# Self-attention over image pixels on one core: shift rows sent from other queues

## The reference

```python
xf = x.reshape(B, Cc, N)                      # x: (4, 256, 32, 32), so N = 1024
q = jnp.einsum('oc,bcn->bon', Wq, xf) + bq[None, :, None]     # 32 x 1024
k = jnp.einsum('oc,bcn->bon', Wk, xf) + bk[None, :, None]     # 32 x 1024
v = jnp.einsum('oc,bcn->bon', Wv, xf) + bv[None, :, None]     # 256 x 1024
scores = jnp.einsum('bqi,bqj->bij', q, k)
attn = jax.nn.softmax(scores, axis=-1)
out = jnp.einsum('bcj,bij->bci', v, attn)
return out.reshape(B, Cc, W, H) + x
```

## Time and profile before

| | us |
|---|---|
| median of 3 runs (lowest, highest) | 170.4 (170.19, 170.5) |
| the profiled execution | 170.36 |
| its span, first to last instruction | 168.5 |
| TensorE matmul busy | 160.3 (95%) |
| VectorE busy | 138.5 (82%) |
| ScalarE busy | 107.2 (64%) |
| GpSimd busy | 49.7 (29%) |

### The profile page before, as it was taken

The page is one execution under the profiler, slowest core; times in us unless marked ns, Lnnn a source line. Parts: engine busy times, 40 slices in busy tenths (PEclk is TensorE's granted clock), DMA queues, the critical chain, the costliest instruction groups (busy, mean ns, idle before and its releaser), DMA issues. The chain is left out here.

```text
span 168.5 us, 2430 instructions
## 1 busy us (share of the span) xinstructions
PE 160.3 (95%) x786; PEld 131.1 (78%) x786; DVE 138.5 (82%) x220; ACT 107.2 (64%) x196; POOL 49.7 (29%) x65
## 2 busy tenths in 40 slices
PE   7978999999999999999999999999999999999990
PEld 5567978797887898798787898798787898767870
DVE  1879899898979999899979999897979879854552
ACT  3658896836997646757896646736895636755210
POOL 6399630170235300420235300420235300214300
PEclk9999999999999999999999999999999999999999
DMA  5932465063312030251311130251311130003003
GB/s 182 352 120 78 128 196 224 0 156 83 131 44 66 28 124 0 51 138 52 124 47 57 41 126 0 55 134 47 127 48 55 42 124 0 5 0 124 0 0 126
DMA packets 7949, 14.48 MB, mean 86 GB/s; under 512 B 1672, under 2 KB 2240, under 8 KB 7936
## 3 DMA queue, kind: packets, MB, share of 16 engines
q1 hardware_dynamic: 6656, 13.37, 24.4%
q0 software_dynamic: 864, 0.82, 2.3%
q10 hardware_dynamic: 416, 0.13, 0.3%
HBM read 4.59 MB, written 4.19 MB: 52 GB/s over the span
## 5 line engine op out<-in xcount | busy, mean ns | idle before, releaser
L818 PE MATMUL acc<-w_hi,v_hi 128*128 128x512 f32 x128 | 51.2, 400 | 0.0
L818 PE MATMUL acc<-w_hi,v_lo 128*128 128x512 f32 x128 | 50.4, 393 | 0.0
L439 ACT ACTIVATE w_full<-st 128x512 f32<-128x512 f32 x64 | 37.8, 592 | 10.5 <-PE st L804 10.5
L406 ACT ACTIVATE dump<-slot,negmax 128x1024 f32<-128x1024 f32 x29 | 32.4, 1118 | 12.8 <-DVE negmax L548 12.4
L826 PE MATMUL acc<-w_lo,v_hi 128*128 128x512 f32 x120 | 38.7, 398 | 0.4 <-POOL w_lo L326 0.2
L603 DVE TENSOR_TENSOR w_lo<-w_full,w_hi 128x512 fp32r<-128x512 f32 x48 | 33.2, 693 | 5.7 <-ACT w_full L439 1.9
L548 DVE TENSOR_REDUCE negmax<-slot 128x1 f32<-128x1024 f32 x29 | 35.3, 1217 | 1.8 <-PE slot L739 1.8
L326 POOL TENSOR_TENSOR w_lo<-w_full,w_hi 128x512 fp32r<-128x512 f32 x16 | 20.7, 1291 | 47.5 <-ACT w_full L439 47.4
L818 PEld LDWEIGHTS acc<-w_hi,v_hi 128*128 128x128 f32 x128 | 24.2, 189 | 7.1 <-DVE x_sb L612 1.2
L818 PEld LDWEIGHTS acc<-w_hi,v_lo 128*128 128x128 f32 x128 | 24.2, 189 | 5.3
L826 PEld LDWEIGHTS acc<-w_lo,v_hi 128*128 128x128 f32 x120 | 22.3, 188 | 7.0 <-POOL w_lo L326 2.1
(11 more groups left out here) (84 smaller groups left out, 187.9 us busy)
## 6 DMA issues: line engine op xcount, KB each, us to landing
out<-x_sb SPq DMA_DIRECT2D x7, 512.0 KB, 2.8
x_sb<-x SPq DMA_DIRECT2D x3, 1024.0 KB, 5.5
k_b<-k_a SPq DMA_DIRECT2D x8, 192.0 KB, 2.5
q_b<-q_a SPq DMA_DIRECT2D x8, 192.0 KB, 2.6
k_a<-qk_parts SPq DMA_DIRECT2D x12, 64.0 KB, 2.2
q_a<-qk_parts SPq DMA_DIRECT2D x12, 64.0 KB, 2.3
x_sb<-x SPq DMA_DIRECT2D x1, 512.0 KB, 3.6
x_sb<-x SPq DMA_DIRECT2D x2, 256.0 KB, 4.8
```

The source lines that it names most:

```text
L406: nc.scalar.activation(dump[:, t % 2, :], s_home(b, t), ACT.Exp, bias=negmax[:, t:t + 1], accum_out=rowsum[:, t:t + 1]).then_inc(rowsum_re ...
L439: nc.scalar.activation(w_full[:, r, :], st[:, j % 2, :], ACT.Exp).then_inc(exp_done, 1)
L818: nc.tensor.matmul(acc[:, c, :], v[:, b % 2, j, ch], w_hi[:, r, :], start=(j == 0 and v is v_hi), stop=False)
```

## The change

The rows of a first half are sent by SyncE, between its two k_b copies. The rows of a second half stay with GpSimd. In the last turn, ScalarE sends the HI row of the second half, after the exponential of tile 5 of that turn (n = 53), and GpSimd only the LO row. A new semaphore, last_row_in, tells of ScalarE's row; TensorE waits for both there.

```diff
+        last_row_in = sem("last_row_in")
...
+        def send_rows(engine, b, h, parts=(HI, LO), done=None):
+            engine.wait_ge(shift_turned, 2 * b + h)
+
+            if b:
+                engine.wait_ge(st_ready, PER * (b - 1) + JT * h + JT)
+            for part in parts:
+                engine.dma_start(
+                    q_b[SHIFT + part:SHIFT + part + 1, cols(h)].bitcast(fp32).rearrange("o (q n) -> o q n", n=P),
+                    shift_rows[part:P:SQUARE, h, :]).then_inc(done or row_in[h], DMA)
...
                 second_stack(k_b, k_a, 0, kb_in[0])
+                send_rows(sp, b + 1, 0)
                 sp.wait_ge(st_ready, PER * b + PER)
...
                 if n % PER == JT:
                     if more:
                         second_blocks(b + 1, 0)
-                    send_rows(b, 1)
+                    send_rows(pool, b, 1, (HI, LO) if more else (LO,))
                     if more:
                         second_blocks(b + 1, 1)
-                if n % PER == JT + 5 and more:
-                    send_rows(b + 1, 0)
                 split_w(n)
...
                     if b == 0 and s == 0:
                         sum_exp(0, TH)
+                    before, t, image = front(b, s - 2)
+                    if before == S and t == JT - 1 and b + 1 == BATCH:
+                        send_rows(act, b, 1, (HI,), last_row_in)
...
                 if j == 0:
                     if b == 0 and h == 0:
                         pe.wait_ge(row_put, 1)
+                    elif b == BATCH - 1 and h == 1:
+                        pe.wait_ge(row_in[h], rows_in(b, h) - DMA)
+                        pe.wait_ge(last_row_in, DMA)
                     else:
                         pe.wait_ge(row_in[h], rows_in(b, h))
```

More of the change, by code:

```diff
@@ L335, in prepare_x1 @@
                                         x_hi[:, 1, :, quarter(i)].bitcast(fp32), ALU.subtract).then_inc(x1_split, 1)
[L338 to L345, removed]
             for half, (parts, made) in enumerate(((wqk_hi, wqk_cut), (wqk_lo, wqk_split))):
```

## The result

The changed kernel takes 169.98 us (median of 22 runs, 169.29 to 170.48); the kernel before, run beside it on the same chip, 170.75 (22 runs, 170.19 to 171.76; the three runs shown ahead had given 170.4). The ratio is 0.9942 with a 95% interval of 0.9926 to 0.9957: faster by 0.74 to 0.43%, which is 0.73 to 1.26 us. The sign of the forecast held, and so did its account of the first part; in the last turn one of its terms failed. Its time of 169.0 was 0.98 too low, and the measured time lies 0.28 above its range.

What follows compares the result with a forecast made beforehand. TensorE was taken to bound the kernel. Wins of 0.18 + 0.37 + 0.37 + 0.50 = 1.42 us from the profiled 170.36 gave 168.94, forecast as 169.0 us with the runs' median 0.04 above; range 168.4 to 169.7.

Steps and rivals of the forecast that it cites:

- Part 1, the three stops: Tile 13 of turns 0 to 2: TensorE's waits for GpSimd's w_lo vanish, 0.44 + 0.37 + 0.37 = 1.18 us.
- The cover in turn 0: Tile 13, turn 0: w_lo done at 52.4 against 53.30 when TensorE wants it, 0.9 us of cover.
- doesn't do what it says: Rival, chance 0.05: GpSimd's w_lo is late for another reason and starts no earlier; 169.9 us, or 170.4.
- the slower one: Rival, chance 0.03: first halves' rows land late from SyncE, losing from a landing of 2.8 us on; 171.4 us.
- the prediction's estimate of 1.2: Landing time of a first half's row from SyncE, estimated from the skill page: 1.6 - 0.4 = 1.2 us.
- The give-back: Near 81 us, tile 24: DVE is full, so 0.26 of turn 0's 0.44 us returns and 0.18 is kept.
- all of it is kept: Rival, chance 0.2: DVE finds 0.26 us between 54 and 78 us, so nothing is given back; 168.7 us.
- The last turn: Second half's late matmul: HI by ScalarE, issuing for about 0.5 us, removes the whole 0.50 us stop.
- the rival priced it: Rival, chance 0.15: last turn gives nothing, from a landing of 2.1 us or an issue over 0.97; 169.5 us.
- my own chain: Last turn: ScalarE's issue delays tile 54's w_hi, then w_full to 147.03; TensorE's matmul at 147.50 leaves 0.47 us cover.
- The other half of that rival, the landing: Last turn: ScalarE's row lands 0.5 us later than the 2.0 taken; it decides from 2.1 us after the issue.
- The forecast win of 1.42: Whole kernel: 0.18 + 0.37 + 0.37 + 0.50 = 1.42 us faster.

Runs made afterwards that it cites:

- e1: Changed kernel with both rows of every second half on GpSimd again, so only the first halves' rows moved to SyncE; 169.77 us, ratio 0.9934.
- e6: Kernel before with two lines exchanged: GpSimd sends the first halves' rows behind w_lo of tile 13, not ahead of it; 174.29 us, ratio 1.0215.
- e7: As e3, but SyncE sends both rows of the last turn and GpSimd none; 169.53 us, ratio 0.9921.
- e5: As e3, but in turn 1 DVE splits two quarters of x_lo at steps 9 and 10 instead of both at 5; 168.83 us, ratio 0.9887.
- e9: As e3, but in turn 0 DVE splits the first quarter of image 2's x_lo at step 12, not 11; 169.51 us, ratio 0.9914.
- e3: Changed kernel, but SyncE instead of ScalarE sends the last turn's HI row; 169.18 us, ratio 0.9912.
- e4: Changed kernel, but ScalarE sends the second half's HI row in all four turns, GpSimd the LO row; one run, 169.72 us.
- e8: Changed kernel, but ScalarE sends the HI row in turn 0 as well as in the last turn; one run, 170.02 us.
- e10: Changed kernel plus one 2 KB DMA that ScalarE issues in turn 2 into a buffer nobody reads; 169.42 us, ratio 0.9903.
- e11: The edits of e5 and e9 together, both x_lo splits later; 169.38 us, ratio 0.9899.
- e2: Changed kernel with the first halves' rows on GpSimd again, so only the last turn's edit remains; 170.6 us, ratio 0.9982.

## Why the forecast was right, and where not

**Part 1, the three stops: right.** All three vanished, 0.44, 0.36 and 0.38 against 0.44, 0.37 and 0.37; e1 shows them alone. The cover in turn 0 was smaller than forecast, since w_lo took 1.61 us and not 1.30: done at 53.45 against 53.97 when TensorE wants it, 0.5 and not 0.9. Nothing hung on that, and SyncE paid nothing for its six issues. That the order on GpSimd was the cause is shown by e6 as well, where w_lo goes first and its stop is gone. The rival "doesn't do what it says" is out, and so is the slower one: the landing on which it rested, 2.8 us and more from SyncE, is about 1.55 (e7). That is within 0.1 of GpSimd's 1.6, so the prediction's estimate of 1.2 is out too. The rule in the Trainium skill, "DMA: Bandwidth & Descriptors", section "Issuing engines are not separate DMA queues", that only the issue time is saved and that it is usually small, holds in its first half; the time saved was worth up to 0.44 us a turn here, because it stood ahead of an operation with no slack.

**The give-back: right, nearly in size.** Forecast 0.26, measured 0.22, so 0.22 of turn 0 was kept and not 0.18. DVE had no room between 54 and 80 us: e5 gives it some, and 4.64 goes back to 4.41. e9 does the same by a different edit, further upstream. The rival "all of it is kept" is out for this change; it took one more edit to make it true.

**The last turn: wrong, and this is the step that failed.** The prediction said of ScalarE that it "issues for about 0.5", from its own first DMA of the run, 0.46 us, and SyncE's 0.51. It took 1.07. I had written the point from which the case turns, an issue longer than 0.97, and given it 0.15; but the rival priced it at the whole 0.50, where by my own chain only the part beyond 0.97 is lost, plus what the wait itself costs. What followed is the chain that I had worked out, with the longer term in it: w_hi of tile 54 starts at 146.22 and not at about 145.6 on this execution's clock, its w_full, the first of the pair at 146.71, ends 0.59 later at 147.30, and the matmul that reuses its bank goes at 147.36 instead of 147.17. A second, smaller loss lies behind it: after this wait the next matmul starts 0.34 later and not 0.23 to 0.24. The two, 0.19 and 0.10, are the 0.29 that is missing: of the 0.50, 0.21 came (5.80 to 5.59). e3, e4, e8 and e10 each bring the issue to 0.56 or less, or off ScalarE, and each shows 5.30 or 5.31: the whole 0.50. The other half of that rival, the landing, was not the cause: in the trace of the changed kernel the last update of last_row_in stands at 146.66, 1.62 us after ScalarE's issue began, and GpSimd's row landed at 146.89, both well ahead of 147.36. I had the margin wrong there as well, but on the safe side, 2.0 us for about 1.6.

**The time and the range.** The forecast was 0.98 us too low. 0.35 of it is the base: 22 runs of the kernel before give 170.75, where the three runs gave 170.4, and the sum was put against those. 0.29 is the last turn, less 0.04 of smaller give-back. The rest, about 0.4, has no place in the traces: from tile 12 to 63 they show 1.19 us won, the ratio says 0.99 (0.73 to 1.26), the two medians 0.77. The forecast win of 1.42 lies outside the ratio's interval; with the last turn and the give-back as measured it is 1.17, and that lies inside. What can be seen besides is that the phase before the turns varies from one profiled execution to the next. The first matmul on q_b and k_b starts between 19.69 (e1) and 20.91 us (e11) in the thirteen profiles, whose order of work up to there is the same; at 19.74 in that of the kernel before, near the early end, and at 20.49 in that of the changed kernel. What is late is the input. On ScalarE the split of the first image waits for the third DMA of x, in the kernel before and in the changed one:

```profile
6.84 0.63 ACT L392 ACTIVATE x_hi<-x_sb 128x512 fp32r<-128x512 f32 x1 [0.65 <-DMA x_sb<-x]
```

```profile
7.60 0.63 ACT L393 ACTIVATE x_hi<-x_sb 128x512 fp32r<-128x512 f32 x1 [1.33 <-DMA x_sb<-x]
```

In e11 it starts at 8.02. 6.84, 7.60 and 8.02 here go with 19.74, 20.49 and 20.91 there, always 12.9 us on. The DMA is issued at 1.65 in all three, and no instruction that the change moves runs before 51 us. So the changed kernel's late start of 0.75 in its profiled execution is that of an input transfer, and it hides part of the gain in that execution's total. How the starts fell in the other 21 runs isn't on record. In e1 the ratio gives more than the stretches (1.13 against 0.90), in the changed kernel less. My range allowed 0.3 for the spread of the base, from three runs that lay within 0.31 of each other; the 22 spread over 1.57.

## What to carry to other kernels

Ask of every DMA issue what stands right behind it on its engine: 1.17 us of issues cost 0.44 a turn because an operation with no slack stood there, and cost nothing on a queue with an idle engine. Here the idlest engine was the better place than a computing one (e3 against the change); keep such an issue early (issued 1.5 us later, beside large copies, the same rows cost 1.3 to 1.8 us a turn more than on SyncE), and if a computing engine must issue on the critical path, let it have issued once before. After removing a stop, look for the next place with no slack: half of turn 0's gain came only after DVE had been given room 27 us later.

## What the runs showed of the hardware

- **ScalarE's first row DMA in mid-program takes twice as long to issue.** 1.07 (after), 1.08 (e2), 1.074 (e4), 1.081 (e8) and 1.09 us (e10's spare copy); every later one 0.50 to 0.55, even after 110 us without one. ScalarE's DMA at the very start of the program took 0.46 and doesn't spare the next one the long issue. What is done in the extra half microsecond isn't visible, and the cause stays open. The traces show no instruction transfer with it: between 33 and 35 us of e4, around its long issue, packets ran on the two data queues q0 and q1 alone, and so in e8.
- **A small transfer from GpSimd's queue lands a microsecond later in large company.** 1.6 us in quiet, 2.5 to 2.65 beside SyncE's 192 KB copies (e6). That it is the company is read from the times of issue, and no run changes the company alone. DVE's two-input operations at the same time are not it: two of them (145.69 to 146.98) ran beside the last rows of the kernel before, which landed after 1.6.
- **A 2 KB row from SyncE lands about 1.55 us after its issue begins** (e7), from ScalarE about 1.6 (the change, whose issue took 1.07 of them), from GpSimd 1.6.
- **DVE and GpSimd hinder each other on SBUF by what DVE reads.** GpSimd's w_lo: 1.30 us undisturbed, 1.29 beside DVE's reduction of a PSUM slot (e9), 1.61 beside DVE's x_lo split with two SBUF inputs (after, e6). DVE's cast: 0.42 undisturbed. Beside w_lo it takes what it must to end 0.28 to 0.30 us after w_lo's end: 1.78 us before, with w_lo's end at 91.58; 0.66 in the changed kernel, with w_lo's end at 90.90; 0.67 in e9, with 52.96. The Trainium skill, "SBUF — State Buffer", section "SBUF: two separate sides", describes a port pair that one of the two holds for a whole instruction, a DVE operation with two SBUF inputs being among those that need it; the trace agrees in who is hindered for the x_lo split, and the cast's fixed distance from w_lo's end fits a wait and not a slower pace. By an exclusive lock w_lo, begun 0.46 before the split's end (51.63 + 0.67 - 51.84), could lose up to 0.46; it lost 0.31. The cast, too, ends 0.12 to 0.14 sooner behind the end that it waited for than its 0.42. The rows' starts alone don't tell who holds the ports: in turn 1 of before the cast's row begins 0.19 ahead of w_lo's, and the cast is the one that waits. In a profile such a wait is a long duration and not an idle gap.
